# A gated four-layer network on one core: one normalisation of the latents for two, and the probabilities' product in two halves

## What is computed

```python
x = x + tanh(g_xattn[1]) * L1_xattn(ctx_1024, layernorm(x), ...)

def L1_xattn(x, latents, gamma_x, beta_x, gamma_l, beta_l, Wq, Wkv, Wo):
    xn = layer_norm(x, gamma_x, beta_x)          # (x - mu) * rsqrt(var + 1e-5) * g + b
    ln = layer_norm(latents, gamma_l, beta_l)
    q = (ln @ Wq)                                # 8 heads of 64
    k_x, v_x = split(xn @ Wkv);  k_l, v_l = split(ln @ Wkv)
    k_x = rope(k_x)
    sim = q k^T * scale over the 256 keys [k_x ; k_l]
    return (softmax(sim) @ [v_x ; v_l]) @ Wo
```

## Time and profile before

| | |
|---|---|
| median of 3 runs | 928.29 us (928.29, 928.73, 923.62) |
| span of the profiled execution | 909.0 us, from its first to its last instruction |
| own time of the profiled execution | not recorded beside its span; the three runs are 14.6 to 19.7 us over the span |
| PE busy | 777.9 us, 86% |
| DVE busy | 599.4 us, 66% |
| ACT busy | 504.2 us, 55% |
| POOL busy | 414.8 us, 46% |
| mean granted clock of TensorE | 0.901 |
| the latent attention | from about 224 us to about 473 us of the span |

### The profile page before, as it was taken

The page is one execution under the profiler, slowest core; times in us unless marked ns, Lnnn a source line. Parts: engine busy times, 40 slices in busy tenths (PEclk is TensorE's granted clock), DMA queues, the critical chain, the costliest instruction groups (busy, mean ns, idle before and its releaser), DMA issues. The chain is left out here.

```text
span 909.0 us, 21425 instructions
## 1 busy us (share of the span) xinstructions
PE 777.9 (86%) x6462; PEld 591.8 (65%) x6462; DVE 599.4 (66%) x1816; ACT 504.2 (55%) x1391; POOL 414.8 (46%) x720
## 2 busy tenths in 40 slices
PE   3999996898679999999979977999969768669991
PEld 1566664798456778777747763666659546449991
DVE  5899995344567889888655447799947727633333
ACT  1577774676256776677635633677754422226663
POOL 3247766000534556765450018466217806824541
PEclk9999997999799999999989986799989775569996
DMA  8999941432000000100004431000000331122214
GB/s 254 384 401 404 289 195 35 90 90 57 23 7 14 14 15 24 26 22 11 19 25 100 114 85 28 16 23 23 2 1 2 98 102 41 46 54 64 74 51 153
DMA packets 69278, 78.96 MB, mean 87 GB/s; under 512 B 12848, under 2 KB 58560, under 8 KB 68912
## 3 DMA queue, kind: packets, MB, share of 16 engines
q1 hardware_dynamic: 59072, 62.15, 21.4%
q0 software_dynamic: 6368, 13.38, 5.1%
q10 hardware_dynamic: 3728, 2.07, 0.9%
HBM read 31.61 MB, written 45.96 MB: 85 GB/s over the span
## 5 line engine op out<-in xcount | busy, mean ns | idle before, releaser
L330 POOL DMA_INDIRECT routed_region<-routed_lines,line_slots x96 | 96.5, 1005 | 27.5 <-issue 23.6
L362 POOL DMA_INDIRECT late_results<-routed_region,line_slots x64 | 63.4, 990 | 77.4 <-remote 61.3
L774 ACT ACTIVATE probs_keymajor<-banks 128x512 f32<-128x512 f32 x128 | 70.2, 595 | 40.4 <-PE banks L584 40.4
L1401 PE MATMUL banks<-exps,work 128*128 128x128 f32 x624 | 85.5, 282 | 5.2 <-ACT exps L1475 5.0
L265 POOL TENSOR_TENSOR small<-small,half_and_eps 128x1 f32<-128x1 f32 x144 | 82.0, 569 | 11.3
L550 PE MATMUL banks<-work 32*128 32x512 f32 x256 | 80.9, 711 | 4.2 <-DVE exps L667 3.2
L658 DVE TENSOR_REDUCE small<-banks 128x8 f32<-128x1024 f32 x64 | 77.6, 1212 | 7.9 <-PE banks L550 3.9
L1401 PEld LDWEIGHTS banks<-exps,work 128*128 128x128 f32 x624 | 77.8, 196 | 7.5 <-ACT exps L1475 7.3
L667 DVE TENSOR_TENSOR exps<-banks,small 128x1024 f32<-128x1024 f32 x64 | 77.7, 1214 | 0.3
L584 PE MATMUL banks<-consts,exps 128*128 128x128 f32 x512 | 74.7, 294 | 1.1 <-ACT work L805 1.1
L584 PEld LDWEIGHTS banks<-consts,exps 128*128 128x128 f32 x512 | 61.1, 152 | 19.2 <-issue 13.0
(11 more groups left out here) (277 smaller groups left out, 1888.3 us busy)
## 6 DMA issues: line engine op xcount, KB each, us to landing
routed_region<-mid SPq DMA_DIRECT2D x52, 528.0 KB, 5.5
exps<-routed_region SPq DMA_DIRECT2D x125, 66.0 KB, 1.9
routed_region<-work SPq DMA_DIRECT2D x86, 64.0 KB, 1.8
weights_f<-in_weights_f SPq DMA_DIRECT2D x1, 4096.0 KB, 18.0
weights_f<-in_weights_f SPq DMA_DIRECT2D x3, 1024.0 KB, 10.9
shifted_rows<-work SPq DMA_DIRECT2D x16, 128.0 KB, 1.7
work<-expert_results SPq DMA_DIRECT2D x8, 256.0 KB, 5.0
routed_region<-routed_lines,line_slots POOLq DMA_INDIRECT x96, 2.4
```

The source lines that it names most:

```text
L330: nc.gpsimd.indirect_dma_start(k.regions[layer % 2], bass.IndirectOffsetOnAxis(k.slots[:, b, j:j + 1], 0), k.line[:, b % LINES, j, :], Non ...
L362: nc.gpsimd.indirect_dma_start(k.late[:, b % 2, j, :], None, k.regions[layer], bass.IndirectOffsetOnAxis(k.slots[:, b, j:j + 1], 0)).then_ ...
L774: nc.scalar.activation(k.pT[:, g * 512:(g + 1) * 512], bank[:, PT + g % 2, :], ACT.Copy).then_inc(s.pT, 1)
L1401: last = nc.tensor.matmul(bank[:, 2 + m % 4, i * T:(i + 1) * T], tile.weights[:, m % COPIES, i * 128:(i + 1) * 128], tile.gotT[:, m % 2, : ...
```

## The change

The second normalisation is folded into the first. A normalised row has mean 0 and variance v/(v+e), so both rounds together are (x - mu) / sqrt(v(1+e) + e*e), with e = 1e-5. `stats_x`, `dev_x`, `norm_x` and `xh` go, `norm_l` reads `k.x` itself and writes `lh` from the statistics of `k.x`, and POOL's add becomes one `tensor_scalar` with a multiply and an add (`twice=True`). The stages `norm_latent` on DVE and `dev_latent` on POOL go. The waits on `s.xh` become waits on `s.lh`. On PE, `pv` becomes two stages, `pv(0)` for the pairs of heads 0 and 1, `pv(2)` for 2 and 3, both of lag 2. `pv(0)` stands where `pv` stood, `pv(2)` behind the logits and ahead of `values(1)`.

```diff
-def layer_norm_steps(nc, k, sem, st, mv, rstd):
+def layer_norm_steps(nc, k, sem, st, mv, rstd, twice=False):
...
-        nc.gpsimd.tensor_tensor(rstd[:, s, 0:1], mv[:, s, 1:2], k.half[:, 1:2], ALU.add).then_inc(sem.var_eps, 1)
+        if twice:
+            nc.gpsimd.tensor_scalar(rstd[:, s, 0:1], mv[:, s, 1:2], 1.0 + EPS, EPS * EPS, ALU.mult,
+                                    ALU.add).then_inc(sem.var_eps, 1)
+        else:
+            nc.gpsimd.tensor_tensor(rstd[:, s, 0:1], mv[:, s, 1:2], k.half[:, 1:2], ALU.add).then_inc(sem.var_eps, 1)
...
-    stats_x, dev_x, norm_x = layer_norm_steps(nc, k, sx, *norm_scratch(k.small, 96))
-    stats_l, dev_l, norm_l = layer_norm_steps(nc, k, sl2, *norm_scratch(k.small, 128))
+    stats_l, dev_l, norm_l = layer_norm_steps(nc, k, sl2, *norm_scratch(k.small, 128), twice=True)
...
-            def pv(b, sl):
+            def pv(p0):
+                def stage(b, sl):
+                    pv_pairs(b, sl, p0)
+                return stage
+
+            def pv_pairs(b, sl, p0):
                 wait(pe, s.pT, b * 4 + 4)
                 wait(pe, s.v, 2 * b + 2)
-                for p in range(L1P):
+                for p in range(p0, p0 + 2):
...
-                last.then_inc(s.pv, 1)
+                if p0:
+                    last.then_inc(s.pv, 1)
...
-                      (probs(0), 2), (k_lat, 0), (probs(2), 2), (next_T, 4), (query, 0), (pv, 2), (values(0), 0),
-                      (logits, 4), (values(1), 0), (ranks, 5), (shared_up, 3), (shared_gate(1), 4)])
+                      (probs(0), 2), (k_lat, 0), (probs(2), 2), (next_T, 4), (query, 0), (pv(0), 2), (values(0), 0),
+                      (logits, 4), (pv(2), 2), (values(1), 0), (ranks, 5), (shared_up, 3), (shared_gate(1), 4)])
...
             def norm_in(b, sl):
-                wait(dve, s.lh, b - 1)
-                norm_x(dve, xh[:, sl, :], at(k.x, b), sl, b + 1).then_inc(s.xh, 1)
                 wait(dve, s.inT, b - 1)
+                norm_l(dve, lh[:, sl, :], at(k.x, b), sl, b + 1).then_inc(s.lh, 1)
                 norm_c(dve, ch[:, sl, :], at(k.ctx, b), sl, b + 1).then_inc(s.ch, 1)
-                wait(dve, s.xh, b + 1)
-                stats_l(dve, xh[:, sl, :], sl, b + 1, s.lh)
-
-            def norm_latent(b, sl):
-                wait(dve, s.inT, b - 1)
-                norm_l(dve, lh[:, sl, :], xh[:, sl, :], sl, b + 1).then_inc(s.lh, 1)
...
-                       (stats_out, 5), (norm_in, 1), (chosen, 7), (norm_latent, 1), (values, 2), (logits, 6),
+                       (stats_out, 5), (norm_in, 1), (chosen, 7), (values, 2), (logits, 6),
...
-            walk(pool, [(dev_out, 7), (dev_in, 2), (rope_add, 3), (keep, 9), (dev_latent, 2), (counted, 9),
+            walk(pool, [(dev_out, 7), (dev_in, 2), (rope_add, 3), (keep, 9), (counted, 9),
```

More of the change, by code:

```diff
@@ L867, in latent_attention @@
      s.q1, s.v1, s.norm, s.pT, s.oT, s.ptr, s.pv, s.added, s.logits_out, s.out, s.xh2, s.xs2, s.xT2,
-     s.logits, s.inv, s.max, s.nmax, s.xh, s.kept, s.halved) = sems.new("a1", """
+     s.logits, s.inv, s.max, s.nmax, s.kept, s.halved) = sems.new("a1", """
         ch lh v inT q k_ctx k_lat exp scores k1 kvT t1 k3 t2 q1 v1 norm pT oT ptr pv added logits_out
-        out xh2 xs2 xT2 logits inv max nmax xh kept halved""")
+        out xh2 xs2 xT2 logits inv max nmax kept halved""")
     c, cols, bank, w = k.c, k.cols, k.bank, k.work
@@ L880, in latent_attention @@
     m = k.mid
-    ch, xh, lh, xh2, xs2 = (split(m[:, n * 256:(n + 1) * 256], 128) for n in range(5))
+    ch, lh, xs2 = (split(m[:, n * 256:(n + 1) * 256], 128) for n in (0, 2, 4))
     mx = split(k.small[:, 0:16], L1H)
@@ L885, in latent_attention @@
     inv = split(k.small[:, 48:64], L1H)
-    sc, sx, sl2, so = (norm_names(sems, "a1_" + n) for n in ("ctx", "x", "lat", "out"))
+    sc, sl2, so = (norm_names(sems, "a1_" + n) for n in ("ctx", "lat", "out"))
     routing_names(sems, "a1", s)
@@ L1063, in add @@
                 wait(dve, s.out, b + 1)
-                wait(dve, s.xh, b + 1)
+                wait(dve, s.lh, b + 1)
                 nc.vector.scalar_tensor_tensor(at(k.x, b), bank[:, MB, 0:D], tg, at(k.x, b), ALU.mult,
@@ L1069, in stats_in @@
                 add_late(dve, b)
-                stats_x(dve, at(k.x, b), sl, b + 1, s.xh)
+                stats_l(dve, at(k.x, b), sl, b + 1, s.lh)
                 stats_c(dve, at(k.ctx, b), sl, b + 1, s.ch)
             def norm_in(b, sl):
-                wait(dve, s.lh, b - 1)
-                norm_x(dve, xh[:, sl, :], at(k.x, b), sl, b + 1).then_inc(s.xh, 1)
                 wait(dve, s.inT, b - 1)
+                norm_l(dve, lh[:, sl, :], at(k.x, b), sl, b + 1).then_inc(s.lh, 1)
                 norm_c(dve, ch[:, sl, :], at(k.ctx, b), sl, b + 1).then_inc(s.ch, 1)
-                wait(dve, s.xh, b + 1)
-                stats_l(dve, xh[:, sl, :], sl, b + 1, s.lh)
-            def norm_latent(b, sl):
-                wait(dve, s.inT, b - 1)
-                norm_l(dve, lh[:, sl, :], xh[:, sl, :], sl, b + 1).then_inc(s.lh, 1)
             def stats_out(b, sl):
@@ L1112, in dev_in @@
             def dev_in(b, sl):
[L1113 removed]
+                dev_l(pool, sl, b + 1)
                 dev_c(pool, sl, b + 1)
[L1116 to L1117 removed]
             def dev_out(b, sl):
```

3 lines of the change are left out of this document (removed).

## The result

| | before | changed |
|---|---|---|
| median (range, runs) | 924.74 us (916.85 to 933.92, 16) | 931.98 us (927.56 to 940.57, 16) |
| ratio to before, 95% interval | | 1.0095 [1.0071, 1.0119] |
| span of the profiled execution | 909.0 us | 933.3 us (its own time 935.08 us) |

The change made the kernel slower by 0.95%, where 920.3 us and a gain were forecast.

The account below looks back on a forecast made before the run. PE was taken to come near to setting the latent attention's pace, the exponentials 0.46 us behind. Terms 6.4 (split product) plus 1.6 (front) gave 8.0 us off the 928.3 us median: 920.3 us, range 915 to 925.

Parts of the forecast that it names:

- The stall that was to go (term of 6.4 us): Latent attention: splitting the probabilities' product ends the second value product's wait for DVE's copy; 14 steps gain 0.46 us each.
- "Nothing gains" from POOL's earlier gathers and scatters: POOL's two fetches and two sends run 2.5 us or more earlier; data wanted a step later, so worth nothing.
- W: Experiments' theory, not the prediction's: the first value product's copy waits, through two value buffers, for the probabilities' product's second half.
- The front (1.6 us): Single normalisation lets PE's first transposes start at 234.11 instead of 235.71: 1.6 us, bounds 1.0 and 1.9.
- I take the difference as the same before and after: Base: runs lie 14.6 to 19.7 us above the 909.0 us span; gain subtracted from the median, 928.3 us.
- B: Rival: every change of tile shape drains PE; a step gains only 0.15 us, total 924.6 us; chance 0.16.
- A: Rival: PE's low clock at the front ends sooner, up to 4.6 us more gained, 915.7 us; chance 0.12.
- D: Rival: PE's low clock at the front lasts through two more steps, 8.4 us slower, 936.7 us; chance 0.04.
- E: Rival: a wait in the queue keeps the old order in effect, no gain, 928 us; chance 0.02.
- The signs that I had set for being wrong: Latent attention: a step over 12.8 us, or another wait than the exponentials' last at the scores.

Follow-up runs that it names:

- after_third: The changed kernel unedited, run on chip 13: 910.48 us, 1.0014 of the kernel before on that chip.
- ring3: The changed kernel with three value buffers instead of two, on chip 5: 900.84 us, 0.9963 of the kernel before.
- norm_only: The changed kernel with the probabilities' product back in one piece, so only the single normalisation, on chip 15: 932.43 us, 1.0063 of before.
- after_again: The changed kernel unedited, profiled a second time, on chip 15: 933.53 us, 1.0076 of the kernel before.
- before_again: The kernel before, unedited, for a second profile, on chip 15: 926.72 us, ratio 1.0027.
- ring3_third: The changed kernel with three value buffers instead of two, on chip 4: 919.30 us, 0.9864 of the kernel before.
- sends_third: The changed kernel with POOL's scatters moved ahead of the rotary sums, on chip 4: 922.87 us, 0.9929 of the kernel before.

## Why the prediction was wrong

**The stall that was to go (term of 6.4 us).** The step that failed is "The copy starts 1.16 after the first product ... so at 336.54 + 1.04 + 1.91 = 339.49, while PE arrives at 339.87. The stall goes with 0.4 to spare." I took the copy's start from the trace of before, where it waits for the value product last, and did not list its other wait, on the signal of the probabilities' product. That signal used to be raised ahead of the first value product, so it never showed in a profile; the change moved it behind. In after_third the copy starts 2.39 behind the first value product instead of 1.16, and the second value product 3.14 behind it instead of 1.91. With the first half at 1.03 where the whole product took 1.90, that is 4.17 against 3.81: 0.36 longer a step, where 0.46 shorter was forecast. ring3 took away that wait (and ACT's like it) and nothing else, and its step is 12.64 against the 12.63 of the prediction. So the sum of the step was right, and the missing wait is what made it fail.

**"Nothing gains" from POOL's earlier gathers and scatters.** They moved by the 2.5 us that I had read. I asked who wants their data, and not what they lie beside. On the chips with lateness this is the larger loss: 7.7 us in the stretch for norm_only. From the third step on, after_again takes 192.54 us against before_again's 181.75: of these 10.8 us W is 4.4, as on chip 13, and 6.4 are lateness that the kernel before does not have. In the changed kernel the step shown in the low-clock rows (first value product at 328.68, the next at 345.16) takes 16.48, 3.03 over 13.45: 1.55 since the second value product starts 4.69 behind the first instead of 3.14, and 1.47 for the low clock, as from there to the keys L943 it takes 338.51 - 333.37 = 5.14 instead of 359.61 - 355.94 = 3.67 in after_third. Over the seven steps the waits cost 10.9 us (7 times 1.55) and the low clock, in five of them, about 7.7.

**The front (1.6 us)** was mis-sized by little at the first transposes: 1.4. The low clock that then lasted longer took about 0.5 of it back in the first two steps. POOL's new instruction took 0.19, as taken.

**The base.** "I take the difference as the same before and after": the 14.6 to 19.7 us between the span and the runs are not time outside the span. In every other profiled run span and time are 1.8 us apart (935.08 and 933.3), so the run behind the span of 909.0 took about 911. Its steps show a kernel without late completions; on chips 5 and 13 before has medians of 908 to 911 us, on 15 and 4 of 925 and 931, as the three runs had. The stretch alone differs by 11.9 to 12.7 us (210.40 and 211.19 against 198.49), and the first `in_T` comes 4.1 and 8.3 us later (239.80 and 243.99 against 235.71), for a reason that was not looked for. A span so far under all timed runs was a sign that the profile did not show what the times were made of.

**The rivals.** B (drains at each change of tile shape) falls: it wanted steps of 12.94, and ring3's are 12.64. There the value products start 1.03 and 1.02 us behind their halves, where 1.04 was taken, and no idle time stands ahead of a half. The Trainium skill, page TensorEngine Tiling (Array Packing), section Tiling Modes, has a change of the mode drain the engine; the rows of ring3 show no more for it than what was in those 1.04. A and D spoke of the low clock at the front. D happened in small: the low clock reached into the second step, for about 0.5 us and not for two whole steps more. The rest of the low clock came later, behind the long waits. E was nearest, "a wait in the queue keeps the old order in effect": a wait did undo the reordering, though not on PE, and I priced it at no loss. None of the five had a loss in a steady step at full clock. The signs that I had set for being wrong are those that came: a step of more than 12.8 us, and another wait last at the end of it.

## What to carry to other kernels

When a stage is split or moved, list every signal that it raises and who waits for each, at what distance: a wait that never shows in the profile, since it is always satisfied, becomes the last one when its signal moves behind the waiter's other work. A reordering that overlaps two products often wants one buffer more, and is to be tried with it: here the same change loses 0.8% to 0.9% with two value buffers where completions are late and nothing that the runs can tell (0.1%) where they are not, and with three it gains 1.0% to 1.4% in three comparisons and 0.4%, not clear of noise, in a fourth. And a profile that is 15 us under all timed runs is to be explained before it is used as a base, by comparing its steps with those of a second profile.

## What the runs showed of the hardware

Completions of TensorE reach other engines late on some chips while POOL issues indirect transfers in a row. With four in a row it is 1.73 us in the profile of the changed kernel (product ended at 347.44, copy at 349.17), against 0.12 in the same kernel on chip 13, and 1.2 to 1.9 us in all disturbed steps of the kernels with two value buffers, where the waiter goes on 0.7 to 1.1 us behind the end of the fourth transfer. A completion beside the third of the four is 1.3 to 1.4 us late (ring3_third), and beside a row of two DVE goes on 0.43 us behind the product on chip 4 (sends_third), 0.03 on chip 5. The waiter is DVE in some kernels and ACT in others.

Chips 15 and 4 showed it in every profile with four in a row, chips 5 and 13 in none. What in the chip holds the completions back was not found, and the records do not tell a signal that is sent late from an engine that takes it up late; the profile gives most of the long waits as "remote".

The same program is 14 to 23 us slower on the chips with lateness (924.75 and 930.85 us against 907.78 to 911.19), of which about 12 lie in this one stretch.

An idle wait of 2.4 us on TensorE was followed by about 3 us at the granted clock 0.50 in five of seven steps of the changed kernel, which cost about 1.5 us each time. The waits of 0.86 us in after_third were not: the clock stayed at 1.00 in all those steps.
